# Decoder on one core: the first attention's MLP loop with the next unit's upward products ahead of the downward ones

## The reference

```python
combined = jnp.concatenate([attn_t, kerple_t], axis=-1)
hdn = jax.nn.gelu(jnp.dot(combined, w1) + b1, approximate=False)
refined = jnp.dot(hdn, w2) + b2
scores = scores + kerple[None] + refined          # refined turned back to head-major
scores = jnp.where(causal[None, None], scores, -jnp.inf)
weights = jax.nn.softmax(scores, axis=-1)
```

## Time and profile before

| | us |
|---|---|
| median of 3 runs | 4821.28 |
| lowest and highest | 4809.44, 4825.56 |
| the profiled execution, its own time | 4790.67 |
| span of the profile | 4788.6 |
| busy: PE, DVE, ACT, POOL | 3996.3, 2440.5, 1681.8, 201.6 |
| mean granted clock of TensorE | 0.919 |

### The profile page before, as it was taken

How to read it: one execution, slowest core, us unless ns; L and a number is a source line. 1 busy time by engine, 2 the same in 40 slices (tenths; PEclk the granted TensorE clock), 3 DMA queues, 4 the chain that set the end, 5 groups by cost and what they waited for, 6 DMA issues and landing times.

```text
span 4788.6 us, 58527 instructions
## 1 busy us (share of the span) xinstructions
PE 3996.3 (83%) x22594; PEld 1893.8 (40%) x22594; DVE 2440.5 (51%) x6012; ACT 1681.8 (35%) x2506; POOL 201.6 (4%) x227
## 2 busy tenths in 40 slices
PE   6777778999876877899977687789997769778998
PEld 2342334345334233435533424333553432433355
DVE  4556645632354765563235476556323556655532
ACT  2544423421253442242126254224213626422511
POOL 1000030000000003000000001200000000110000
PEclk9898989999989898999988899899998889889999
DMA  5222033022413103402241400340214140034031
GB/s 191 78 75 40 16 69 72 7 83 69 139 46 93 20 16 69 78 1 89 63 148 41 96 12 16 69 78 1 96 58 146 45 102 1 16 69 78 1 102 54
DMA packets 146417, 304.75 MB, mean 64 GB/s; under 512 B 15012, under 2 KB 86692, under 8 KB 139172
## 3 DMA queue, kind: packets, MB, share of 16 engines
q1 hardware_dynamic: 146120, 300.80, 24.2%
HBM read 231.53 MB, written 69.21 MB: 63 GB/s over the span
## 4 chain that ended last, share of the span: by engine, by line
PE 62%; DVE 16%; ACT 7%; DMA 6%; issue 3%; POOL 3%; SPq 2%; POOLq 0%; DVEq 0%
PE ps L1064 10%; PE ps L511 6%; DVE mx L641 6%; PE ps L494 5%; PE ps L1082 5%; PE ps L437 5%; PE ps L1385 3%; DMA qparts<-QP 2%; ACT a_X L1454 2%; PE ps L499 2%; PE ps L333 2%; PE ps L442 2%; PE ps L1303 2%; DVE c_V L908 2%; DMA QS<-qparts 2%
## 5 line engine op out<-in xcount | busy, mean ns | idle before, releaser
L641 DVE TENSOR_REDUCE mx<-ps 128x1 f32<-128x512 f32 (+3 forms) x1280 | 771.0, 646 | 535.0 <-PE ps L442 273.0
L585 ACT ACTIVATE PT<-ps 128x1024 f32<-128x1024 f32 (+3 forms) x640 | 605.3, 959 | 519.7 <-PE ps L499 296.0
L437 PE MATMUL ps<-KS,QS 96*128 96x512 bf16 (+3 forms) x1280 | 487.5, 403 | 195.8 <-DMA QS<-qparts 119.2
L1064 PE MATMUL ps<-xnT,f_w 128*128 128x512 f32 x1088 | 488.7, 592 | 0.0
L494 PE MATMUL ps<-QS,KS 99*128 99x512 bf16 (+2 forms) x1280 | 424.3, 376 | 6.7 <-ACT QS L575 6.2
L511 PE MATMUL ps<-PT,VP 128*32 128x512 f32 (+3 forms) x2560 | 379.5, 580 | 1.6
L1162 DVE TENSOR_TENSOR f_tm<-f_si,ps 128x512 f32<-128x512 f32 x128 | 88.1, 688 | 499.6 <-ACT f_si L1114 499.5
L437 PEld LDWEIGHTS ps<-KS,QS 96*128 96x128 bf16 x1280 | 129.7, 102 | 487.8 <-DVE mx L641 277.8
L1114 ACT ACTIVATE f_si<-ps 128x512 f32<-128x512 f32 x136 | 80.9, 598 | 604.0 <-PE ps L1077 584.9
L1064 PEld LDWEIGHTS ps<-xnT,f_w 128*128 128x128 f32 x1088 | 206.4, 190 | 203.7 <-issue 197.1
L333 PE MATMUL ps<-mneg,identb 128*128 128x512 bf16 x800 | 196.3, 403 | 97.4 <-issue 49.0
(11 more groups left out here) (241 smaller groups left out, 5560.0 us busy)
## 6 DMA issues: line engine op xcount, KB each, us to landing
f_w<-in_wF SPq DMA_DIRECT2D x136, 384.0 KB, 3.1
VP<-in_v_unit SPq DMA_DIRECT2D x12, 2048.0 KB, 11.5
KS<-kparts SPq DMA_DIRECT2D x96, 256.0 KB, 9.9
QS<-qparts SPq DMA_DIRECT2D x144, 128.0 KB, 5.2
scores<-a_fin SPq DMA_DIRECT2D x64, 256.0 KB, 3.1
a_fin<-scores SPq DMA_DIRECT2D x16, 1024.0 KB, 8.0
a_Y<-in_wA SPq DMA_DIRECT2D x5, 3072.0 KB, 15.0
scores<-a_fin SPq DMA_DIRECT2D x64, 192.0 KB, 2.9
```

The source lines that it names most:

```text
L437: last = nc.tensor.matmul(o, m["QS"][0:KR, h, i * P:(i + 1) * P], m["KS"][0:KR, h, f:f + w], start=True, stop=plain)
L585: nc.scalar.activation(m["PT"][:, mp % 2, j % 2, :, 0:w], ps[:, b0:b0 + 2, 0:w], ACT.Exp, scale=HD ** -0.5).then_inc(g("exp"), 1)
L641: nc.vector.tensor_reduce(m["mx"][:, h % 2, i, f // BANK:f // BANK + 1], ps[:, k % 2, 0:w], AX.X, ALU.max, negate=True).then_inc(g("slot_f ...
L1064: last = nc.tensor.matmul(ps[:, 2 * v + e % 2, :], m["w"][:, e % NRING, (2 * v + k) * P:(2 * v + k + 1) * P], xnT[:, k, :], start=(k == 0) ...
```

## The change

TensorE's loop puts `up(k + 1)` ahead of `down(k)`, but for the units listed in `DOWN_FIRST`, those before a chunk of one unit: 15 to 20. ScalarE's `weights(c - 1)` stands after the Gelu of the last unit of chunk c instead of the first, VectorE's `normal(c - 1)` after `refined` of the last unit, and the turns of chunk c are spread over the units from `FIRST[c + 2]` to `FIRST[c + 3] - 1`. For chunks of one unit, and the turns of the chunks before two of them, these places are the same as before. The number of instructions stays.

```diff
             for c in range(NCHUNK):
-                units = range(FIRST[c + 1] + 1, FIRST[c + 2] + 1)
+                units = range(FIRST[c + 2], FIRST[c + 3])
                 n = len(A_TURNS[c])
...
+        DOWN_FIRST = [FIRST[c + 1] - 1 for c in range(NCHUNK - 1) if FIRST[c + 1] == LAST[c + 1]]
...
             for k in range(NU + 4):
-                if k < NU:
+                if k in DOWN_FIRST:
                     down(k)
-                if k + 1 < NU:
                     up(k + 1)
+                else:
+                    if k + 1 < NU:
+                        up(k + 1)
+                    if k < NU:
+                        down(k)
                 for y in range(BANKS_TO[k], BANKS_TO[k + 1]):
...
-                if k == FIRST[c] and c:
+                if k == LAST[c] and c:
                     weights(c - 1)
             weights(NCHUNK - 1)
...
-                if k in FIRST[1:NCHUNK + 1]:
-                    normal(FIRST.index(k) - 1)
+                if k in LAST[1:]:
+                    normal(LAST.index(k) - 1)
+                if k == NU:
+                    normal(NCHUNK - 1)
```

## The result

The changed kernel takes 4753.91 us (median of 6 runs, 4744.81 to 4777.96), the kernel before 4812.88 over six runs beside it (4798.36 to 4825.56). The ratio is 0.9888, 95% interval 0.9855 to 0.9921: 54 us faster by the ratio, 59.0 by the two medians. The second comparison's 4767.11 would have fallen inside it.

What follows compares the result with a forecast made beforehand. No engine is full in the MLP loops; TensorE and ScalarE taking turns over one unit's banks set the pace. Terms sum to -8.2 us a loop, -33 in four, from the 4821.28 median to 4788 us, range 4762 to 4816.

Steps and rivals of the forecast that it cites:

- Part 1: Units 0 to 3: `down` leaves the chain and runs under the next Gelu; 28.7 to 21.8 us, -6.9 a loop.
- part 2: Units 4 to 11: gaps without exponentials hold `up` alone, between full and half clock; 46.9 to 40.1 us, -6.8 a loop.
- Part 3: Units 11 to 15, weighted values of query tile 3: TensorE-bound, first block waits as long or longer; +1 us a loop.
- Part 4: Handover to one-unit chunks, units 15 to 18: later load of chunk 10 +2.8, turns +0.7; +3.5 us a loop.
- Part 6: Rest of the loop from unit 18: old order, only the clock's pattern can differ; +1 us a loop.
- Part 5: Loads 4 to 9: issued later and wanted sooner, but still landing in time; cost zero, cover 3.1 us instead of 15.
- Nothing given back: Rival, chance 0.20: the front gains 13.7 us a loop and the handover finds other cover; 55 us, time 4766.
- The clock: Rival, chance 0.16: TensorE runs `up` at half clock after waits behind exponentials; loop gains 2.8 us, -11 in all, 4810.
- The late loads: Rival, chance 0.07: loads before `up` of chunks 4 to 10 come too late; +11 us a loop, +43, 4864.
- The table loads: Gaps with exponentials: the skill's 2.66 us a switch would add 2.8 a pair, gain nothing, 4821; given no chance.

Runs made afterwards that it cites:

- changed again: The changed kernel itself timed and profiled once more, no edit, beside the kernel before; 4767.11 us against 4813.30, ratio 0.9916.
- five slots alone: Changed kernel plus a fifth slot for the chunks' scores, so a load waits for the turns of the chunk five before; ratio to before 0.9840.
- all three: Changed kernel with a fifth score slot, chunk 6's exponentials, scaling and turns at their former places, and unread products in TensorE's waits; ratio to before 0.9799.

## Why the prediction was wrong

By its own parts, in us a loop, against the first profile and the second:

| part | forecast | changed | changed again |
|---|---|---|---|
| 1, Gelu 0 to 4 | -6.9 | -7.1 | -7.4 |
| 2, Gelu 4 to 11 | -6.8 | -6.7 | -6.1 |
| 3, Gelu 11 to 15 | +1 | +0.3 | +0.9 |
| 4, Gelu 15 to 18 | +3.5 | +2.0 | +1.8 |
| 6, from Gelu 18 | +1 | -0.4 | +0.2 |
| sum | -8.2 | -12.0 | -10.7 |

- **The mechanism and the front were right.** `down` left the chain, the gaps of 512 columns without exponentials became 4.1 to 5.9 us, those with them stayed at 7.5, and parts 1 and 2 gave 13.8 us for 13.7 (13.5 in the second profile). That it fits so closely is in part luck. Part 1 was reckoned from the first round's 28.7 us where the mean of four is 28.1, and its new time of 21.8 was too long by about as much (21.0 and 20.7). And the middle that part 2 took between full and half clock is an average of rounds that lay from 38.6 to 43.0 us.
- **The terms that failed are those of what is given back: parts 4 and 6.** Part 4 put +2.8 us for the load of chunk 10, as `up(18)` starts that much later. In the first round it did start 2.5 us later (3.7 after the end of Gelu 17 against 1.2), with a wait of 2.52 us for the load, but the gap from Gelu 17 to Gelu 18 grew only by 1.9 us in the mean of the rounds, from 6.7 to 8.6 (8.4 in the second profile). In the kernel before, `up(18)` took 3.5 us at half clock and ended just with ScalarE's own 6.7 us of Gelu, exponentials and table loads (ScalarE idled some 0.1 us); here it took 3.1, part of it at full clock, and ScalarE idled 2.10. Wrong too was the +0.7 on top for the turns: gaps 15 to 16 and 16 to 17 were 6.7 and 7.1 us (before 6.6 and 7.1), since they are ScalarE's own work and the turns lie under it. So part 4 came to +2.0 and +1.8 instead of +3.5. Part 6 put +1 us for a clock pattern with no mechanism behind it; it was -0.4 and +0.2, with a granted clock of 18-21 of 0.98 to 0.99 in the first profile against 0.95 to 1.00 before. Part 3 was 0.1 to 0.7 high: the wait before the values did grow, from 3.38 to 4.13. Together these terms were +5.5 and measured +1.8 and +2.9. In four loops that is 11 to 15 us.
- **The base.** I applied the difference to a median of 4821.28 of three runs. Over six runs the median of the same kernel was 4812.88, and 8.4 us of the 34 between 4788 and 4753.91 come from that. The range's low end had 4 us for the spread, less than this shift alone.
- **The rest.** Of the 34 us the loops make 15 (47.9 for 32.8) and the base 8.4; about 11 are open. By the ratio the first comparison gives 54 us for 47.9 in the loops, the second 40 for 42.6, so they lean to opposite sides, and no run shows a gain outside the loops. The six runs of the changed kernel go with the mean granted clock: four of 4744.81 to 4755.43 us at 0.921 to 0.922, two of 4777.38 and 4777.96 at 0.915. That the median fell among the four is part of why it lies so low; that the clock is the cause is not shown.
- **Part 5 was right.** The four waits of `up` for a load in the first loop (12.0 us) are those of `up(0)`, `up(18)`, `up(20)` and `up(21)`; none is of chunks 4 to 9.
- **The rivals.** Nothing given back, 55 us, was near the first result; its reason (that other cover is found) was half right: the load's wait of 2.5 to 2.8 us was there, but the gap grew by 1.9 only. The clock: the granted clock of 4 to 11 was 0.89 in three rounds and 0.82 in one before, and 0.82 to 0.87 after, as that rival had it, but less time stood under it. In two rounds of the second profile it was 0.75, under the 0.8 that the prediction had named as a sign of being wrong, and these rounds gained some 4 us of the 6.8. So the rival was at work in part of the rounds. Its own sum had a slip: it took +4.5 us for what is given back, where parts 3, 4 and 6 add to +5.5; with that it is -7 us, 4814. The late loads were real in one place, not in seven.
- **The table loads.** The exponential starts 1.30 us after the start of the load (144.81 and 146.11), as before, and a gap with exponentials is still 7.5 us. The drain of 1.38 us that the Trainium skill names behind a load (ScalarE: Activation LUTs, What ACT_TABLE_LOAD costs) is not seen in the changed kernel either.

## What to carry to other kernels

Where a single buffer passes between two engines, look for work on either that stands between its release and its refill, and put it behind the refill; then move everything that depends on the delayed work by the same step. Done by halves the change gave 5.2 of 12.0 us, or nothing, as the next wait in a stream held up the very work that had been brought forward. Price what is given back as strictly as what is gained: work that lies under the other engine's own in a gap (here the turns) costs nothing, and a term without a mechanism ("the clock's pattern") doesn't belong in the sum, only in the range.

## What was not expected

The code outside the loops is the same in the kernel before and the changed one, yet its share of a profiled span was 3986.3 us (before), 3988.3 (changed) and 4006.6 (changed again). Over all profiles it went up to 4019.8 (all three, with 14 unread products ahead of each loop). That is a spread of 20 to 33 us, more than the 14 us of loop time between five slots alone and all three. The traces show where it lies. From the end of the first loop to the second, the kernel before took 982.7 us and the one with chunk 6 at its old places 1000.6. VectorE was busy 494.8 us in both and ScalarE 310.9 and 310.5, but TensorE 846.7 and 862.7, at a granted clock of 0.93 and 0.91. So it is the same work of TensorE at another clock; what sets the clock from run to run stays open. The loops themselves repeat to a few us, 754.4 and 759.7 in sum. Changes of this size are read from the stretch that they touch.
